# GNN layer pair on one core: second half's edge rows multiplied as they land, sixteen row buffers, indices copied by ScalarE

## The reference, cut to what matters

```python
seg = edge_type * n + dst
agg = jax.ops.segment_sum(x[src], seg, num_segments=N_REL * n)
cnt = jax.ops.segment_sum(ones, seg, num_segments=N_REL * n)
mean = agg.reshape(N_REL, n, -1) / jnp.maximum(cnt, 1.0).reshape(N_REL, n, 1)
h1 = jnp.einsum('rni,rio->no', mean, W_rel) + x @ W_root + b_rgcn
xw = h1 @ W_gcn
...
out = jax.ops.segment_sum(xw[src] * norm[:, None], dst, num_segments=n)
out = out + xw * (dinv * dinv)[:, None]
return out + b_gcn
```

## Time and profile before

| | us |
|---|---|
| median of 3 runs | 3916.02 (3913.81 to 3950.95) |
| profiled execution | 3912.97 |
| its span, first to last instruction | 3911.2 |
| PE busy | 3508.4 (90%) |
| DVE busy | 2004.9 (51%) |
| ACT busy | 1449.5 (37%) |
| POOL busy | 1417.5 (36%) |

### The profile page before, as it was taken

The page is one execution under the profiler, slowest core; times in us unless marked ns, Lnnn a source line. Parts: engine busy times, 40 slices in busy tenths (PEclk is TensorE's granted clock), DMA queues, the critical chain, the costliest instruction groups (busy, mean ns, idle before and its releaser), DMA issues.

```text
span 3911.2 us, 67870 instructions
## 1 busy us (share of the span) xinstructions
PE 3508.4 (90%) x19011; PEld 2237.3 (57%) x19011; DVE 2004.9 (51%) x4523; ACT 1449.5 (37%) x2473; POOL 1417.5 (36%) x1878
## 2 busy tenths in 40 slices
PE   6889977958999999999999999999999987667778
PEld 4334457857566666666666666666666654444445
DVE  7999997856522122122123454454454326666564
ACT  2765534625122222222223444444443323333330
POOL 0760000000055544444303444444443206677661
PEclk9999977979999999999999999999999997778889
DMA  2000000011143333333334555555544434444441
GB/s 81 1 1 0 0 10 1 1 36 56 58 145 102 103 113 103 102 113 103 101 115 138 157 163 166 167 164 166 162 159 143 141 120 140 123 127 125 127 105 55
DMA packets 224476, 390.32 MB, mean 100 GB/s; under 512 B 38885, under 2 KB 179172, under 8 KB 224398
## 3 DMA queue, kind: packets, MB, share of 16 engines
q1 hardware_dynamic: 164942, 246.72, 18.6%
q0 software_dynamic: 57600, 141.81, 13.4%
q10 hardware_dynamic: 1856, 0.79, 0.1%
HBM read 250.79 MB, written 138.41 MB: 100 GB/s over the span
## 4 chain that ended last, share of the span: by engine, by line
PE 70%; DVE 14%; issue 6%; DVEq 2%; ACT 2%; DMA 2%; another core or an unknown queue 2%; POOL 1%; SPq 0%; ACTq 0%; POOLq 0%
PE bank L1554 17%; PE bank L1556 17%; PE bank L1555 17%; PE bank L1438 3%; PE bank L1545 3%; PE bank L1546 3%; PE bank L1611 3%; DVE arena L1001 3%; PE bank L1529 2%; DVE arena L1037 2%; PE bank L1332 1%; DVE arena L1000 1%; PE bank L1621 1%; DVE agg_lo L1207 1%
## 5 line engine op out<-in xcount | busy, mean ns | idle before, releaser
L1554 PE MATMUL bank<-arena 128*128 128x384 f16 (+1 forms) x4200 | 1384.5, 330 | 3.1 <-issue 2.2
L1555 PE MATMUL bank<-arena 128*128 128x384 f16 (+1 forms) x4200 | 1382.2, 329 | 4.1 <-issue 4.1
L1556 PE MATMUL bank<-arena 128*128 128x384 f16 (+1 forms) x4200 | 1381.2, 329 | 3.4 <-issue 3.4
L811 ACT ACTIVATE arena<-bank,winv 128x384 f32<-128x384 f32 (+1 forms) x680 | 391.0, 579 | 1327.1 <-PE bank L1556 967.8
L573 POOL DMA_INDIRECT arena<-y_half,idx_now x720 | 764.7, 1062 | 284.5 <-issue 174.4
L1554 PEld LDWEIGHTS bank<-arena 128*128 128x128 f16 (+2 forms) x4200 | 425.9, 101 | 285.6 <-issue 34.5
L1556 PEld LDWEIGHTS bank<-arena 128*128 128x128 f16 (+2 forms) x4200 | 425.5, 101 | 272.1 <-issue 16.1
L1555 PEld LDWEIGHTS bank<-arena 128*128 128x128 f16 (+2 forms) x4200 | 426.2, 101 | 265.0 <-issue 15.3
L801 ACT ACTIVATE agg_hi<-arena,typ_s 128x384 fp32r<-128x384 f32 x720 | 406.8, 608 | 446.4 <-remote 138.2
L1207 DVE SCALAR_TENSOR_TENSOR agg_lo<-arena,typ_s,agg_hi 128x384 fp32r<-128x384 f32 x720 | 442.3, 614 | 159.4 <-ACT agg_hi L801 80.1
L1545 PE MATMUL bank<-agg_hi,agg_oh 128*128 128x384 f32 x720 | 307.7, 427 | 179.0 <-DVE agg_lo L1207 137.5
(11 more groups left out here) (213 smaller groups left out, 3646.4 us busy)
## 6 DMA issues: line engine op xcount, KB each, us to landing
y_half<-arena SPq DMA_DIRECT2D x612, 192.0 KB
arena<-in_L_gnn_W_rel_dram SPq DMA_DIRECT2D x68, 1152.0 KB
arena<-y_half,idx_now POOLq DMA_INDIRECT x720
y_half<-arena SPq DMA_DIRECT2D x68, 147.0 KB
w_now<-rel_inv_dram,idx_now POOLq DMA_INDIRECT x360, 2.7
arena<-in_x_dram SPq DMA_DIRECT2D x10, 384.0 KB, 3.5
arena<-in_L_gnn_b_rgcn_dram SPq DMA_DIRECT2D x10, 384.0 KB
x_dram<-arena SPq DMA_DIRECT2D x9, 384.0 KB, 2.6
```

What stands on the lines that cost most here:

```text
L811: nc.scalar.activation(to, bank[n % RB][0:r, 0:CH], ACT.Copy, scale=winv[0:r, c:c + 1]).then_inc(r_copied, 1)
L1554: nc.tensor.matmul(acc, xh, w_hi[c][:, k, :], start=(k == 0), stop=False)
L1555: nc.tensor.matmul(acc, xh, w_lo[c][:, k, :], start=False, stop=False)
L1556: ins = nc.tensor.matmul(acc, xl, w_hi[c][:, k, :], start=False, stop=(k == KT - 1))
```

## The change

The first half's edges keep the five steps. For the second half the tail becomes:

- DVE makes a one-hot that already holds the edge weight, in full 32-bit floats (`tail_onehot`), into eight slots. There is no high and low part any more, so L801 and L1207 have no counterpart.
- PE multiplies this one-hot with the landed rows, one 32-bit matmul per block (`tail_sum`), and waits for the landing itself.
- The rows have sixteen buffers: `graw`, the four `ybuf` of the stage before, and four that lay under `x1t`. A gather waits for `e_sum`, 16 blocks back, once for two gathers (`FREE`).
- ACT copies the indices (`next_index`), six units ahead, for both halves; POOL copies none.
- Since `x1t` lies under row buffers, SP loads `x1` after the last `edge_add` instead of at the start of the tail.

```diff
+        tail_rows = graw + ybuf + [view(afterV + 2 * D * 4 + i * CH * 4, [CH]) for i in range(UT)]
+        tail_oh = [view(afterV + 4 * D * 4 + i * P * 4, [P]) for i in range(2 * UT)]
...
+            sp.wait_ge(e_added, HALVES * UNITS + 2)
             for n in range(NT):
...
             def gather(q, i, m, c):
 
                 V, place, _ = unit(q, i, m, c)
-                pool.wait_ge(idx_copied, i * m + (c + UNITS + q * (UNITS + 1) + 1))
+                pool.wait_ge(idx_next, V + 1)
                 for t in range(UT):
-                    if t == UT - 1:
-                        pool.wait_ge(e_hi, V * UT + UT)
-                        next_rows(q, i, m, c + 1)
-                    pool.wait_ge(e_lo, V * UT + t + 1)
-                    pool.nop(nofuse=True)
+                    if t % FREE == 0:
+                        pool.wait_ge(e_lo, V * UT + (t + FREE))
+                        pool.nop(nofuse=True)
...
+            def tail_gather(i, m, c):
+
+                V = i * m + (c + (HALVES - 1) * UNITS)
+                pool.wait_ge(idx_next, V + 1)
+                for t in range(UT):
+                    if t % FREE == 0:
+                        pool.wait_ge(e_sum, V * UT + (t + FREE + UT - len(tail_rows)))
+                        pool.nop(nofuse=True)
+                    k, loaded, _ = tail_slot(i, m, c, t)
+                    nc.gpsimd.indirect_dma_start(
+                        out=tail_rows[k], out_offset=None, in_=y_dram[HALVES - 1],
+                        in_offset=bass.IndirectOffsetOnAxis(ap=idx_now[:, c % IDXB, t:t + 1], axis=0)).then_inc(loaded, 16)
...
+            def next_index(u, c):
+
+                nc.scalar.copy(idx_now[:, c % IDXB, :], idx_y[:, bass.ds(u * UT, UT)]).then_inc(idx_next, 1)
...
+            def tail_index(i, m, c):
+
+                act.wait_ge(e_sum, i * (m * UT) + ((HALVES - 1) * UNITS + c + 2) * UT)
+                next_index(i * m + (c + IDXB), c)
...
+            def tail_onehot(i, m, c):
+
+                V, place, _ = unit(HALVES - 1, i, m, c)
+                for t in range(UT):
+                    at = bass.ds((i * m + c) * UT + t, 1)
+                    dve.wait_ge(e_sum, V * UT + (t + 1 + UT - 2 * UT))
+                    nc.vector.tensor_scalar(tail_oh[place * UT + t], iota[:, 0:P], dst_s[:, at], w_s[:, at],
+                                            ALU.is_equal, ALU.mult).then_inc(e_oh, 1)
...
+            def tail_sum(i, m, c):
+
+                V, place, _ = unit(HALVES - 1, i, m, c)
+                acc = bank[SUMS + place][:, 0:CH]
+                pe.wait_ge(e_added, V + 1)
+                for t in range(UT):
+                    k, loaded, uses = tail_slot(i, m, c, t)
+                    pe.wait_ge(e_oh, (i * m + c) * UT + (t + 1))
+                    pe.wait_ge(loaded, uses * 16)
+                    nc.tensor.matmul(acc, tail_oh[place * UT + t], tail_rows[k], start=(t == 0), stop=(t == UT - 1))\
+                        .then_inc(e_sum, 1)
```

More of the change, by code:

```diff
@@ L375, in program @@
         CHAIN = 5
-        assert UNITS % (2 * IDXB) == 0 and 2 * PER % IDXB == 0
+        FREE = 2
+        assert UT % FREE == 0
+        assert UNITS % IDXB == 0 and 2 * PER % IDXB == 0 and PART * UT % len(tail_rows) == 0
         def step(q, i, j):
@@ L396, in unit, with tail_slot @@
             return i * m + (c + q * UNITS), c % 2, i * (m // 2) + (c // 2 + q * (UNITS // 2))
+        def tail_slot(i, m, c, t):
+            units = len(tail_rows) // UT
+            assert m % units == 0 or isinstance(i, int)
+            k = c % units * UT + t
+            before = UNITS // 2 if k < 2 * UT else 0
+            return k, (g_loaded + tail_loaded)[k], i * (m // units) + (c // units + before + 1)
         class Count:
@@ L603, in _ @@
             stored(HALVES - 1)
-            next_rows(HALVES - 1, 0, 2 * IDXB, 0)
+            pool.wait_ge(e_lo, UNITS * UT + 2 * UT)
             with pool.Fori(0, UNITS // (2 * IDXB)) as i:
                 for c in range(2 * IDXB):
-                    gather(HALVES - 1, i, 2 * IDXB, c)
+                    tail_gather(i, 2 * IDXB, c)
+            for c in range(UNITS // (2 * IDXB) * 2 * IDXB, UNITS):
+                tail_gather(0, UNITS, c)
             pool.wait_ge(row_loaded, 48)
@@ L824, in _ @@
                     act.wait_ge(edge_w, UNITS)
+                    for c in range(IDXB):
+                        next_index(c, c)
                     with act.Fori(0, AGG_PAIRS) as i:
```

47 lines of the change are left out of this document (25 added, 22 removed).

## The result

In twenty timed runs each, the kernel before takes 3932.6 us in the median (3912.0 to 3956.6) and the changed kernel 3910.3 (3874.3 to 3913.9). The ratio is 0.9931, 95% interval 0.9904 to 0.9958. The forecast was 3808 with a range of 3790 to 3862.

The account below looks back on a forecast made before the run. The prediction took the tail to be bounded by a ring of waits among its engines, with POOL setting the new pace. From 3912.97 us, -103.6 for gathers, -2 for the end and +1 for PE waits gave 3808, range 3790 to 3862.

Parts of the forecast that it names:

- Gathers: Tail, POOL: 1.29 us per gather step, so 464.6 us from first to last gather against 568.2, a gain of 103.6.
- The change frees nothing: Rival, tail: POOL's 79 us of stops have another cause than buffers; time stays within 5 us of 3913; chance 0.02.
- Does the DMA follow?: Tail transfers: 152 GB/s needed, a share of 0.55; sixteen buffers give a 20.6 us ring with 15 us left for lateness.
- The rival of longer gathers: Tail: each DVE one-hot holds up a gather for 0.31 us, step 1.56, whole time 3904 us; chance 0.11.
- nearest suspect: Tail: DVE's work beside the gathers as what draws some out, to a mean of 1.016 us against 0.95.
- PE and its clock: Tail: a 32-bit matmul record takes 0.32 us, PE's work 391 us at full clock, and the clock was taken to hold.
- PE becomes the bound: Rival, tail: PE's clock stays at 0.80 or 0.75, giving 3829 or 3861 us; chance 0.15.
- DVE and ACT: Tail: DVE needs 161 us plus root additions, its one-hots a unit ahead; ACT's 90 index copies of 0.2 us are hidden.
- The end: From the tail's last gather to the next sums: 14.45 us become 12.2, a gain of 2.
- The loads of `x1`: Loads moved behind the last `edge_add`: POOL's additions start some 3 us later but are covered, so cost nothing.
- The first half: Before the tail: ACT gains 96 index copies of 0.2 us, hidden by busy PE; cost nothing, at most 19 us.
- The sum: Whole kernel: -103.6 for gathers, -2 for the end and +1 for small PE waits take 3912.97 to 3808 us.

Follow-up runs that it names:

- first_half: The changed kernel with the tail of the kernel before, except that ScalarE copies the indices and POOL waits once per two gathers: 3800.5 us against 3812.2 of the kernel before.
- after_third: The changed kernel, unchanged, run again beside the kernel before on a chip with prompt news: 3778.2 us against 3819.3, ratio 0.988.
- late_root_2: The changed kernel with VectorE's root additions behind the next unit's one-hots in the tail's first 40 units, on a chip with late news: 3880.8 us, ratio 0.9942.
- ahead: The changed kernel with tail one-hots three units ahead in sixteen slots and four PSUM banks for the sums: 3858.7 us against 3912.1 of the kernel before.
- sp_loads_2: The changed kernel with the tail's gathers replaced by same-size sequential loads from SyncE and no index copies there (sums not right): 3754.6 us.
- no_gather_2: The changed kernel without the tail's gathers after the first sixteen and without their index copies (sums not right): 3728.3 us.

## Why the prediction was wrong

**The step that failed is the reading of the tail's stops**, in "Gathers" and in "The change frees nothing". It took the 79 us of stops in the earlier trace rows for waits on eight buffers, which sixteen buffers would end. In truth the old tail takes 568 or 558 us with late news and by the estimate above 489 with prompt news, 69 to 79 us less. And first_half, which keeps the eight buffers and the split, has less than 5 us of stops in its 470 us where the news is prompt (4 of them, the first gather among them). So nearly all of the stopped time was the lateness of news, and more buffers do not bring news. Against 489 the tail's gain is 37 us, with late news 26 to 29. The sign stood in rows that the prediction quoted and did not use: ACT's group in the earlier trace rows is idle for 134.4 us on PE and for 131.9 on "remote". The prediction named the first number and left the second out.

**"Does the DMA follow?"** counted on 15 us of slack in the ring, since "the longest stop of POOL now is under 5 us". That was circular: the stops were short because POOL, with eight buffers, soon stopped by itself. In the changed kernel the first root addition starts 10.9 us after its product's last matmul (3257.71 to 3268.65), and POOL came to a stop 39 times after the first gather.

**Gathers.** The pace was forecast at 1.29 us and is 1.25. A gather takes 954 ns where 1016 was measured before. The index copies did not draw it out, since first_half has none on POOL and 1004 ns. It goes with the split: in the trace of the kernel before the 239 gathers that overlap an `agg_lo` (L1207) take 1.04 us in the mean, the other 120 take 0.955. That was the prediction's nearest suspect. The 359 steps of after_third are 13 us less than the sum had. The rival of longer gathers (step 1.56) is refuted. By the rule of the Trainium skill (page SBUF — State Buffer, section Who interferes with whom) each of the 360 one-hots, 357 ns long, could have kept GpSimd from writing descriptors; no run here shows it, and the mean of 954 ns beside them decides against it for this instruction, which reads 16-bit and writes 32-bit numbers: in after_third the 147 gathers that overlap a one-hot take 0.957 us, the other 212 take 0.945.

**PE and its clock.** Right where the news is prompt: a record at 0.32 us, 0.97 to 0.99 granted against 0.75 and 0.83 in the earlier trace rows. Under late news 0.89 and 0.92 at 72% and 85% busy: since the same kernel has no stops and 0.97 to 0.99 with prompt news, the lower clock comes with the stops. The rival "PE becomes the bound" (3829 to 3861) is not what happened: PE waits in both cases.

**DVE and ACT.** The index copy takes 0.193 us on ScalarE (0.2 forecast). The one-hot takes 0.36 and not 0.31. That they "stand a unit ahead" was true and too little under late news, but late_root_2 and ahead (527.2 and 524.6 us against 532.1 and 539.5) show that more lead gives back 15 us at most.

**The end.** 14.45 us were forecast to become 12.2; they are 16.6 (3781.62 to 3798.17) and 13.5 with prompt news (3651.07 to 3664.54). **The loads of `x1`** cost nothing, as forecast: the stretch behind the next sums' start is 112.0 us in each profile of the changed kernel, 111.98 in the earlier trace rows. **The first half** cost nothing either, from first product to tail: with prompt news 2125 to 2126 us in each profile with its gathers (the kernel before has none), with late news 2143.5 and 2136.0 before against 2130.8 to 2137.2 after.

**The sum.** In the profile's terms: forecast 464.6 us from first to last gather, less 14 for the pace (449 where 463 stood), more 87 for the stops behind the first gather and 2 of smaller delays, are 539.5, 75 too many; the first product to the tail gained 6; the end lost 4 against its forecast. From 3808 that leads to about 3881, and the lower group of the changed kernel is at 3874 to 3880. The profile of 3912 has the longer sort stage on top. So the forecast had the terms of the kernel after the change nearly right for prompt news (3777 to 3778 there) and took them off a time with late news. "The change frees nothing" said "within 5 us of 3913", and the profile agrees with it by chance only.

## What to carry to other kernels

When engines wait, list what ends their waits, and look at the share that ends on "remote" or "issue" behind finished work before any of it is booked as want of buffers: where GpSimd gathers, a stop can be late news of a finished matmul, and more buffers took little of it away here (524.6 us of ahead against 539.5 and 532.1). Plain loads of rows in sequence, issued by SyncE, had no such stops (sp_loads_2). Before the gain of a change is forecast from one profile, find the stages that it cannot touch and compare only executions in which they are equal.

## What the runs showed that was not expected

On two of five chips every kernel of this study had much of PE's news late while GpSimd gathered, in the tail and in both stages ahead of it (root counts up to 13.9 us behind the last matmul's start, in late_root_2, where 0.34 is prompt), and on three of them never. The kernel before takes 3896 to 3912 us with late news (3912 to 3918 in the first comparison, late too by both its profiles) and 3812 to 3820 with prompt news, in the group of the shorter sort stage. In no_gather_2 the lateness goes with the last gather (4.81 us, then 0.63). Late increments of several matmuls came in one burst: in the changed kernel's profile 206 of `e_sum` follow the one before by 42 or 43 ns, where PE starts these matmuls 0.64 us apart or more. And the sort stage takes 175 or 204 us from execution to execution of one kernel: in the longer kind (the changed kernel's profile) PE waited 174 times, 28.1 us in all, for GpSimd's one-hots at L548, in the shorter kind (after_third) twice, 0.5 us. What makes it so is open.
